# Paced gathers and a shared in-place product in a fused graph and feed-forward layer

## What is computed

```python
def reference(x, src, dst, ...):          # x: 6250 x 512, 106250 edges, dst sorted
    h0 = layernorm(x)
    agg = segment_sum(h0[src], dst, 6250)             # a sum over each node's edges
    h = h0 @ W_self + b_self + (agg / max(deg, 1)) @ W_neigh
    h = layernorm(h) * gamma + beta
    h = where(h >= 0, h, alpha * h) + h0
    x = x + h
    z = layernorm(x)                                  # feed-forward, 512 -> 1408 -> 512
    gate, up = z @ wq_gate.T, z @ wq_up.T             # ternary weights, a scale for 128 inputs
    return x + (silu(gate) * up) @ wq_down.T
```

## Time and profile before

| | us |
|---|---|
| three runs | 1811.4, 1826.8, 1832.7 |
| median | 1826.8 |
| the profiled execution | 1812.8 |
| its span in the trace | 1811.0 |
| TensorE's mean granted clock | 0.931 |

### The profile page before, as it was taken

One profiled execution on the slowest core, in us unless ns is written; L12 is line 12 of the kernel. 1 busy time (PEld: TensorE's weight loads), 2 busy tenths in 40 slices (PEclk: granted clock), 3 DMA queues, 4 the chain that ended last, 5 costly groups with the idle time before them and its releaser, 6 DMA issues.

```text
span 1811.0 us, 22718 instructions
## 1 busy us (share of the span) xinstructions
PE 1515.5 (84%) x6819; PEld 625.7 (35%) x6820; DVE 1058.9 (58%) x2254; ACT 1182.7 (65%) x2250; POOL 969.2 (54%) x944
## 2 busy tenths in 40 slices
PE   7999978967888889879797898788876877877897
PEld 3454423433332333323233333233332232332343
DVE  8888526544555665554664555547465455473866
ACT  5477300146676777858786686677775876877886
POOL 1623366655556656556675665566656547665000
PEclk9999999987998999989998999899998988998999
DMA  9779488975767777667676777576667657776101
GB/s 284 254 231 273 143 308 272 284 229 151 207 175 222 200 193 219 189 188 216 194 210 184 225 205 197 161 224 190 191 174 211 182 173 200 202 193 173 39 9 40
DMA packets 199788, 353.88 MB, mean 195 GB/s; under 512 B 92380, under 2 KB 94144, under 8 KB 199666
## 3 DMA queue, kind: packets, MB, share of 16 engines
q0 software_dynamic: 70560, 231.27, 44.7%
q1 hardware_dynamic: 129106, 121.15, 22.3%
HBM read 295.79 MB, written 39.62 MB: 185 GB/s over the span
## 4 chain that ended last, share of the span: by engine, by line
PE 62%; issue 12%; ACT 10%; DVE 5%; another core or an unknown queue 4%; DMA 3%; SPq 2%; DVEq 0%; ACTq 0%
PE f_ps L1088 18%; PE f_ps L1089 17%; PE f_ps L879 14%; PE agg_ps L987 10%; ACT f_ps L1183 6%; DMA x1T<-hsx 2%; PE side_ps L1030 1%; ACT acc L1193 1%; ACT hT L1208 1%; DVE acc L1531 1%; DVE nmr L1278 1%; DMA edges<-dst_pad 1%; PE agg_ps L875 1%; DMA node_table<-work 1%
## 5 line engine op out<-in xcount | busy, mean ns | idle before, releaser
L832 POOL DMA_INDIRECT rows<-node_table,idx x882 | 899.9, 1020 | 566.9 <-issue 257.9
L1183 ACT ACTIVATE f_ps<-f_ps,ratio 128x512 f32<-128x512 f32 (+2 forms) x1305 | 773.8, 658 | 344.1 <-PE f_ps L1089 166.6
L1088 PE MATMUL f_ps<-x1T,tern 128*128 128x512 f16 (+2 forms) x1144 | 431.5, 381 | 157.7 <-DMA x1T<-hsx 43.1
L1089 PE MATMUL f_ps<-x1T,tern 128*128 128x512 f16 (+2 forms) x1144 | 429.1, 379 | 3.0 <-issue 3.0
L987 PE MATMUL agg_ps<-rows,hot 128*64 128x512 f16 x2058 | 286.6, 416 | 15.1 <-issue 13.3
L1531 DVE SCALAR_TENSOR_TENSOR acc<-f_ps,scl,acc 128x512 f32<-128x512 f32 (+2 forms) x143 | 102.2, 716 | 297.7 <-PE f_ps L1089 177.8
L1088 PE MATMUL f_ps<-hT,tern 128*128 128x512 f16 (+2 forms) x572 | 220.9, 388 | 50.0 <-issue 23.7
L1088 PEld LDWEIGHTS f_ps<-x1T,tern 128*128 128x128 f16 x1144 | 113.4, 99 | 405.3 <-issue 174.6
L1089 PE MATMUL f_ps<-hT,tern 128*128 128x512 f16 (+2 forms) x572 | 219.3, 386 | 2.1 <-issue 2.1
L987 PEld LDWEIGHTS agg_ps<-rows,hot 128*64 128x64 f16 x2058 | 125.9, 119 | 178.8 <-issue 105.6
L1089 PEld LDWEIGHTS f_ps<-x1T,tern 128*128 128x128 f16 x1144 | 114.5, 100 | 93.1 <-issue 23.2
(11 more groups left out here) (186 smaller groups left out, 1616.7 us busy)
## 6 DMA issues: line engine op xcount, KB each, us to landing
rows<-node_table,idx POOLq DMA_INDIRECT x882
hsx<-own_rows SPq DMA_DIRECT2D x49, 256.0 KB
hsx<-in_x SPq DMA_DIRECT2D x48, 256.0 KB
out_nodes<-work SPq DMA_DIRECT2D x48, 256.0 KB, 2.2
node_table<-work SPq DMA_DIRECT2D x30, 256.0 KB, 4.9
xj<-xnt_rows SPq DMA_DIRECT2D x26, 256.0 KB
acc<-own_rows SPq DMA_DIRECT2D x23, 256.0 KB
own_rows<-acc SPq DMA_DIRECT2D x23, 256.0 KB
```

The costliest lines, as they stand in the source:

```text
L832: pool.indirect_dma_start(out=rows[:, at, :], out_offset=None, in_=table[:, :], in_offset=bass.IndirectOffsetOnAxis(ap=of, axis=0)).then_i ...
L1088: pe.matmul(to, lhs, parts[0], start=g == 0, stop=False, skip_group_check=True)
L1089: pe.matmul(to, lhs, parts[1], start=False, stop=True, skip_group_check=True).then_inc(p_ff, 1)
L1183: act.activation(ps, ps, ACT.Copy, scale=ratio[:, w if up else 2, j:j + 1]).then_inc(a_scaled, 1)
```

## The change

A new list `step_at` holds the tick of each step. `steps_before(t, k)` counts those that stand ahead of a tick, so `p_ff >= steps_before(t, k)` says that TensorE is done with all of them. GpSimd now waits before gather n of block b (n in the order of `ORDER`) for the steps ahead of tick b * 18 + n - 9, beside the wait for its place in the ring. And of the products in ticks of blocks below 49, number 3, 9, 15 and so on (counted in the order of steps) is VectorE's instead of ScalarE's: 199 of 1196. What is computed stays the same.

```diff
     SLOT_OF = {s: t for (t, k), steps in AT.items() for s in steps}
+    step_at = [at for at, steps in AT.items() for s in steps]
...
+    LEAD = 9
+
+    def steps_before(t, k):
+        return sum(at < (t, k) for at in step_at)
+
...
         if not is_last(kind, g):
-            by = False if SLOT_OF[s] < BLOCKS else products % 5 in (1, 3)
+            by = products % 6 == 3 if SLOT_OF[s] < BLOCKS else products % 5 in (1, 3)
             products += 1
...
                 for j in ORDER:
                     after(pool, p_used, freed_by(b, j))
+
+                    after(pool, p_ff, steps_before(*divmod(max(b * STEPS + ORDER.index(j) - LEAD, 0), STEPS)))
                     gather(row_at(b, j), idx[:, b % 4, j:j + 1], gathered[len(BURST_ROUNDS) * (b % 2) + FIRST_USE[j]])
```

## The result

| | before | changed |
|---|---|---|
| three runs, us | 1811.4, 1826.8, 1832.7 | 1751.7, 1755.4, 1757.8 |
| median, us | 1826.8 | 1755.4 |
| the profiled execution, us | 1812.8 | 1751.7 |
| its span, us | 1811.0 | 1749.9 |

The ratio is 0.968 (95% interval 0.963 to 0.974): 3.2% faster, where I had forecast 1801 us and a range of 1765 to 1845. The direction was right; the size was not, and, as the experiments show, the reason wasn't either.

The account below looks back on a forecast made before the run. TensorE bounds, ScalarE's products second. Product gain 46, minus cost 30, plus clock 3, gives 19 us off the profiled 1812.8, so 1794; the median was put at 1801 us, range 1765 to 1845.

Parts of the forecast that it names:

- its 5.1 us: Largest stall ending on a moved product, ScalarE and VectorE both idle; left out, so 16 of 22 us were kept.
- The gathers' pace: GpSimd's gathers spaced by the new wait: fewer bytes at once, worth 0 to the 39 us TensorE waits for x1T; taken 0.
- a sign of being wrong: Prediction called wrong if TensorE's wait for x1T, expected near 39 us, moved by more than 10 us either way.
- The product's gain: TensorE's waits for ScalarE's products shrink as 199 of 1196 move to VectorE: 46 us, between 21 and 96.
- the 127: TensorE's waits before, 61.0 us for ScalarE's product plus 65.8 of "issue", taken as what waits for ScalarE's products are worth.
- The product's cost: Moved products late in VectorE's in-order queue, 23.5 us, and its other work for TensorE pushed back: 2.5 to 53, taken 30.
- VectorE late: Rival: pushes in VectorE's queue don't coincide, +32 us, 1845 to 1859; decides once VectorE's cost passes 46 us; 14%.
- The push on x1T: Chain to x1T pushed 1.7 us at the first chunk edge, at most 0.8 at later ones; taken as nothing, otherwise 10 us.
- The wait for gathers at edges: TensorE waits 2.4 to 3 us for late gathers at three chunk edges, hidden behind x1T's wait: 0, 8 us if uncovered.
- The clock: TensorE's time at 1.2 instead of 2.4 GHz behind stalls shrinks with 16 us less of stalls: 0 to 5, taken 3.

Follow-up runs that it names:

- the first four experiments: Against the kernel before: only VectorE's products 1852.0 us, only the gathers' wait 1752.9, both 1769.0, both with gathers released 18 ticks ahead instead of 9, 1900.4.
- the pair with the wait: Two kernels with the gathers' wait, against the kernel before: all products ScalarE's 1752.9 us (0.952), every sixth product VectorE's 1769.0 us (0.963).
- the 128x160 clearing: Kernel before, but GpSimd clears a 128x160 tile ahead of each gather and waits for it; no wait for steps: 1733.1 us (0.940), again 1727.9 (0.936).
- the products alone: The changed kernel with the gathers' wait for steps taken out, every sixth product still VectorE's: 1852.0 us, 1.010 of the kernel before.
- a lead of 18: The changed kernel with gathers released 18 ticks ahead of their order instead of 9: 1900.4 us, 1.034 of the kernel before.
- only some gathers held: Kernel before with the wait for steps only ahead of gathers 0 to 3 of each block, 1843.8 us (1.017), or only 12 to 17, 1898.9 us (1.036).

## Why the prediction was wrong

**What bounds the kernel.** I had 5.8% of "another core or an unknown queue" in the earlier trace rows, 77 us of the chain, took up the named shares around it and gave this one no price. In the earlier trace rows I saw ScalarE and VectorE idle for 5 us together and wrote that they were "released by something the profile can't name", and kept its 5.1 us out of the sum. That was the step that failed: the late signals had no term, and so the gathers, which bring them on, had none either. GpSimd's rows of the same microseconds would have told what else ran.

**The gathers' pace: 0, "from 0 to the 39 us of x1T".** It is worth 4 to 5% by itself, 92 us in the set of the first four experiments. I had looked for its worth in the transfers' bytes and in the transposes. x1T did fall, 39.1 to 27.4, the smaller part (and by more than the 10 us that I had named as a sign of being wrong), and halving the bytes gave almost nothing. Nor did the gathers come 1.66 us apart: of those in the stretch with sums, 71% still follow the one before within 1.35 us, against 77% before. The wait moves and shortens the rows; it doesn't do away with them. The bounds were no bounds, since they held only the mechanism that I had thought of.

**The product's gain: 46.** 42 us by the count of pauses in the pair with the wait, and in the waits 127 became 89.5 where I had said 80. The size is right there, but the 127 were not ScalarE's queue alone: with all products ScalarE's and the signals on time (the 128x160 clearing) they are 14.2 + 42.3 us in one trace and 30.8 + 49.6 in the other. And in the products alone, without the wait, they hardly fell (113.3 us against 117.1, 370 to 1600).

**The product's cost: 30, "from 2.5 to 53".** 60 us. By that count VectorE's products themselves cost 41, where setting them against VectorE's rows gave 23.5; and 19 came from L1038, which I had left out. VectorE's index and count rows stand behind the added products too, and TensorE waits for them once a block; that this is the reason I infer from the order of the rows. My rival "VectorE late" put the turning point at 46, and it was passed; the products alone came out at 1% slower (interval -0.1 to 2.1%).

**The push on x1T: nothing**, near enough: with the products TensorE waits for x1T 2 us more with the gathers' wait (18.2 to 20.2, 370 to 1600 us) and 6 us more without it (36.3 to 42.5). **The wait for gathers at edges: 0, "8 us if the cover is gone".** It is 24.5 us in five places. I had counted three edges of 2.4 to 3 us behind x1T's wait, but the longest alone is 6.9.

**The clock: 3.** The mean granted clock rose from 0.931 to 0.938. If a stretch is at one of two levels, 1.2 or 2.4 GHz, the share at the lower is twice what is missing to 1: 250 us of the span before, 217 after, and at most half of the 33 us is saved, some 16 (an estimate from the two means, as if TensorE were busy in all of it). I had let it follow 16 us of stalls; many more went.

So it was luck that the forecast came to the right side: its gain, the products', costs time by itself, and the part that decided stood at nothing.

## To carry to other kernels

Price every share of the chain of waits, the unnamed ones first: where two or more engines stand still together with "remote", look at what the remaining engine does in just those microseconds, and measure how late the signals are; the share itself isn't the gain. Where GpSimd issues many indirect transfers in a row, try a little distance between them before moving work between engines; here 1.47 us instead of 1.25 from one to the next, with nothing else changed, was worth 6%. An engine with time to spare in total is not a cheap place for work that others wait for: count also what stands behind the added instruction in its queue, and who waits for that.

## What the runs showed of the hardware

TensorE's signals reached ScalarE and VectorE late, by 6.5 us in the clearest place, while GpSimd issued indirect gathers of 128 rows at one in 1.25 us. TensorE's count of steps itself moved late, while ScalarE's and VectorE's counts kept within 0.02 us of their instructions' ends. The delay was longest behind seven and more gathers in a row (1.70 us on average), the time lost to it did not depend on whether a row was 1 or 2 KB (0.994 of the time without the wait), and two thirds of the long delays went at one gather in 1.47 us (51 and 55 instead of 161). That the gathers' timing brings it on is shown by the runs that change nothing but the clearing between them. By which way is open: I have not separated the making of the descriptors from the DMA engines' handling of them or of their completions, and no run changed the number of rows in a gather. Open as well is why half-measures (a lead of 18, only some gathers held) were slower than no wait; their signals were about as late as without one, which explains the gain that is missing and not the loss.
